# Four output tiles of the seventh image moved from the local step to other PSUM banks and an earlier place in TensorE's program

## What is computed

```python
x = x + L0(gn(x))     # 8 heads, each row of 32 tokens attends to itself
x = x + L1(gn(x))     # one head over all 1024 tokens
# L1: q = x Wq, k = x Wk (32 wide), v = x Wv (256 wide)
energy = einsum('bid,bjd->bij', k, q)
out = gamma * einsum('bij,bjc->bic', softmax(energy), v)
```

## Time and profile before

| | us |
|---|---|
| runs | 690.97, 690.84, 688.51 |
| median of the three | 690.84 |
| profiled execution, whole | 689.47 |
| its span | 687.7 |

### The profile page before, as it was taken

The page is one execution under the profiler, slowest core; times in us unless marked ns, Lnnn a source line. Parts: engine busy times, 40 slices in busy tenths (PEclk is TensorE's granted clock), DMA queues, the critical chain, the costliest instruction groups (busy, mean ns, idle before and its releaser), DMA issues.

```text
span 687.7 us, 15145 instructions
## 1 busy us (share of the span) xinstructions
PE 593.7 (86%) x5859; PEld 429.9 (63%) x5859; DVE 473.2 (69%) x765; ACT 349.5 (51%) x486; POOL 196.9 (29%) x194
## 2 busy tenths in 40 slices
PE   2475587689999999999999999999999999649987
PEld 2254265346877677757775777668776767327756
DVE  4445246868886878687868788688868794664562
ACT  2522425097518852686348652875278513651363
POOL 5602221132046023513342314420460342001203
PEclk9795798599999999999999999999999999879999
DMA  5042132212332332243042323224223132201101
GB/s 160 0 124 62 43 83 82 62 38 64 108 74 66 78 93 71 63 108 93 23 107 76 84 61 92 68 57 112 68 68 82 33 74 64 72 1 39 49 0 62
DMA packets 40308, 47.53 MB, mean 69 GB/s; under 512 B 6848, under 2 KB 32320, under 8 KB 40256
## 3 DMA queue, kind: packets, MB, share of 16 engines
q1 hardware_dynamic: 36960, 43.47, 24.0%
q10 hardware_dynamic: 3296, 3.34, 1.4%
HBM read 10.09 MB, written 8.39 MB: 27 GB/s over the span
## 4 chain that ended last, share of the span: by engine, by line
PE 64%; DVE 16%; ACT 6%; issue 5%; SPq 4%; DMA 3%; POOL 1%; ACTq 0%; DVEq 0%; POOLq 0%
PE pb L253 9%; PE pb L254 8%; PE pb L255 8%; PE pa L253 7%; PE pa L255 6%; PE pa L254 6%; PE pa L491 4%; DVE max_neg L925 4%; PE pb L557 4%; PE pa L464 3%; PE pb L539 3%; SPq L321 3%; DVE ast L827 2%; PE pa L393 2%; PE pb L393 2%
## 5 line engine op out<-in xcount | busy, mean ns | idle before, releaser
L253 PE MATMUL pb<-v_h,e_h 128*128 128x257 f16 x464 | 127.5, 275 | 0.0
L255 PE MATMUL pb<-v_h,e_l 128*128 128x257 f16 x464 | 126.5, 273 | 0.0
L254 PE MATMUL pb<-v_l,e_h 128*128 128x257 f16 x464 | 126.1, 272 | 0.0
L925 DVE TENSOR_REDUCE max_neg<-pb 128x1 f32<-128x1024 f32 x64 | 77.5, 1211 | 55.6 <-PE pb L539 55.1
L940 DVE TENSOR_TENSOR e_l<-e,e_h 128x1024 f16<-128x1024 f32 x64 | 77.8, 1223 | 17.1 <-ACT e L749 15.5
L758 ACT ACTIVATE qk_h<-pb,y_fac 128x256 f32<-128x256 f32 x58 | 27.5, 474 | 109.9 <-DVE y_fac L947 109.6
L1097 POOL TENSOR_TENSOR y<-qk_h,y 128x256 f32<-128x256 f32 x64 | 46.3, 727 | 118.1 <-ACT qk_h L758 118.0
L749 ACT ACTIVATE e<-pb,f_energy 128x1024 f32<-128x1024 f32 x64 | 71.3, 1114 | 16.1 <-PE pb L557 16.1
L1078 POOL TENSOR_TENSOR xb<-xin,bias 128x2048 f32<-128x2048 f32 x8 | 36.7, 4588 | 125.9 <-DVE x L905 125.9
L1083 POOL TENSOR_TENSOR before_turn<-before_turn,a_rinv 128x1024 f32<-128x1024 f32 x16 | 30.6, 1912 | 128.3 <-DVE a_rinv L886 128.3
L253 PE MATMUL pa<-a_nh,wqkv_h 128*128 128x512 f16 x128 | 49.9, 389 | 13.1 <-DVE before_turn L896 7.3
(11 more groups left out here) (136 smaller groups left out, 1373.4 us busy)
## 6 DMA issues: line engine op xcount, KB each, us to landing
xin<-in_x SPq DMA_DIRECT2D x16, 512.0 KB, 4.6
diag<-qkT SPq DMA_DIRECT2D x64, 128.0 KB, 2.3
diag<-turned SPq DMA_DIRECT2D x64, 128.0 KB, 2.4
turned<-before_turn SPq DMA_DIRECT2D x128, 64.0 KB, 2.0
out<-y SPq DMA_DIRECT2D x24, 256.0 KB, 2.1
out<-y ACTq DMA_DIRECT2D x8, 256.0 KB, 2.1
q_stack<-qk_hl SPq DMA_DIRECT2D x8, 128.0 KB, 2.3
k_stack<-qk_hl SPq DMA_DIRECT2D x8, 128.0 KB, 2.4
```

The source lines that it names most:

```text
L253: nc.tensor.matmul(out_ap, lh, rh, start=start, stop=False)
L254: nc.tensor.matmul(out_ap, lh, rl, start=False, stop=False)
L255: return nc.tensor.matmul(out_ap, ll, rh, start=False, stop=stop)
L925: nc.vector.tensor_reduce(max_neg[:, it:it + 1], pb[:, 0:2, :].rearrange("p a n -> p (a n)"), X, ALU.max, negate=True).then_inc(b_max, 1)
```

## The change

Output tiles 0 to 3 of image 6 are no longer made in `first` of step 7 in `pb` banks 2 and 3. They are made in `second` of step 6 in the four banks of `pa`. Tiles 0 and 1 are made key tile by key tile: key tile 0 after `b_energy_T(6, 3)`, 1 after `b_energy_T(6, 4)`, 2 after `b_energy_T(6, 5)`, 3 after `b_energy_T(6, 6)`; key tiles 4 to 6 after the last transposes of image 7 and ahead of `group_mean`; key tile 7 behind `group_mean`. Then tiles 2 and 3 follow: key tiles 0 and 1 still ahead of `group_var`, key tiles 2 to 7 behind it and ahead of `b_project_qk`. Tiles 4 to 7 of image 6 stay in `first` of step 7; tiles 4 and 5 have no wait of their own for a bank, 6 and 7 wait for the scaled results of tiles 4 and 5. `outputs_behind` also waits until image 7's local output has left `pa` (`a_ol`). For image 7, tiles 6 and 7 move from `pa` banks 0 and 1 to `pb` banks 0 and 1, and wait for its last exponential instead of for its scaled tiles 0 and 1.

```diff
@@ result_bank
+        def next_to_last(b):
+            return isinstance(b, int) and b == IMAGES - 2
+
         def result_bank(b, it):
 
             if last_image(b):
-                it = it % 6
-                return pa[:, it, :] if it < 4 else pb[:, it - 2, :]
+                return pa[:, it, :] if it < 4 else pb[:, (it - 2) % 4, :]
+            if next_to_last(b) and it < 4:
+                return pa[:, it, :]
             return pb[:, 2 + it % 2, :]
@@ b_output
                     pe.wait_ge(b_el, nth(b, 8, jts[-1] + 1))
 
                     if it >= 6:
-                        pe.wait_ge(b_part, nth(b, 8, it - 5))
+                        pe.wait_ge(b_exp, nth(b, 8, 8))
+                elif next_to_last(b) and it < 4:
+                    pe.wait_ge(b_el, nth(b, 8, jts[-1] + 1))
+                elif next_to_last(b):
+                    if it >= 6:
+                        pe.wait_ge(b_part, nth(b, 8, it - 1))
                 elif jts[0] == 0:
@@ first, TensorE
-                    if o and not last_image(i - 1): b_output(i - 1, it, b, range(0, 4))
+                    if o and b and not next_to_last(i - 1): b_output(i - 1, it, b, range(0, 4))
                     if b and it == 2: b_energy(i, 1, m)
-                    if o and not last_image(i - 1): b_output(i - 1, it, b, range(4, 8))
+                    if o and b and not next_to_last(i - 1): b_output(i - 1, it, b, range(4, 8))
@@ outputs_behind
-            def outputs_behind(b, jts):
+            def outputs_behind(b, jts, its=range(6)):
 
                 for jt in jts:
                     if jt == 0:
 
                         pe.wait_ge(b_vl, nth(b, 4, 4))
-                    for it in range(6):
+                        pe.wait_ge(a_ol, nth(IMAGES, 2, 0))
+                    for it in its:
                         b_output(b, it, False, (jt,))
@@ second, TensorE
                 if last_image(i): outputs_behind(i, (0,))
+                if next_to_last(i): outputs_behind(i, (0,), (0, 1))
                 if b: b_energy_T(i, 4)
                 if b and f: b_project_v(i, (3,))
                 if last_image(i): outputs_behind(i, (1,))
+                if next_to_last(i): outputs_behind(i, (1,), (0, 1))
                 if f: a_project_qk(i + 2, 1, (1,))
                 if b: b_energy_T(i, 5)
                 if last_image(i): outputs_behind(i, (2,))
+                if next_to_last(i): outputs_behind(i, (2,), (0, 1))
                 if m: a_projection(i + 1, f, (0, 1))
                 if b: b_energy_T(i, 6)
                 if last_image(i): outputs_behind(i, (3,))
+                if next_to_last(i): outputs_behind(i, (3,), (0, 1))
                 if m: a_projection(i + 1, f, (2,))
@@
                 if m: transposes("b", i + 1, (2, 3))
                 for j in range(4):
+                    if next_to_last(i) and j == 0: outputs_behind(i, (4, 5, 6), (0, 1))
                     if m and j == 2: group_var("b", i + 1)
                     if f: a_project_v(i + 2, (j,))
                     if m and j == 0: group_mean("b", i + 1)
+                    if next_to_last(i) and j == 0:
+                        outputs_behind(i, (7,), (0, 1))
+                        outputs_behind(i, (0, 1), (2, 3))
+                    if next_to_last(i) and j == 2: outputs_behind(i, range(2, 8), (2, 3))
```

## The result

| | before | changed |
|---|---|---|
| median of 11 runs each | 688.3 us | 692.79 us |
| lowest, highest | 687.47, 690.97 | 691.28, 696.6 |
| span of the profiled execution | 687.7 | 692.3 |

The ratio is 1.006, with a 95% interval from 1.0043 to 1.0078: the change costs some 4.1 us. The two spans differ by 4.6 us; the working's sum on the span was +3.9.

The account below looks back on a forecast made before the run. TensorE was busy 86%, but step 7's start hung on a DMA chain and the maxima. Terms -1.5 + 4.5 - 1.5 + 2.4 = +3.9 us, on the runs' middle of 690.2: 694.1 us, range 691.0 to 696.5.

Parts of the forecast that it names:

- (a, b): Step 6's first hole: key tiles 0 to 3 of tiles 0 and 1 let the mean come 1.5 us earlier.
- the likeliest case: Step 6's first hole: added key tiles keep the clock full, so the projection's 24 matmuls gain 2.16 us.
- The other bound, 0.5: Step 6's first hole: the clock falls all the same but returns sooner; the mean comes only 0.5 us earlier.
- (c): Image 7's norm: variance matmul queued behind the last split and 18 matmuls at half clock, +4.5 us.
- (d): Behind the variance: 36 matmuls under cover cost nothing, and the query/key projection at full clock gains 1.5 us.
- (e): First half of step 7: without cover TensorE idles 5.4 us, then energies and tile 4 meet half clock; +2.4 us.
- the bound I gave: Step 7, tile 4 all at half clock: 5.1 us, making that stretch's sum +3.2 us.
- (f): From energy 4 on: order unchanged, image 7's tiles 6 and 7 in other banks cost nothing; 0.
- the kept clock in the norm: Rival: filled holes keep the clock full through image 7's norm, 2.6 instead of 4.5 us; sum +2.0, 692.2 us; chance 0.22.
- Full clock everywhere: Rival: norm and step 7's energies 0 to 3 also at full clock; sum -1.5, 688.7 us; chance 0.08.
- the clock falling at both holes: Rival: clock falls in both step 6 holes, part of the 36 matmuls delays the projection; about +6, 696.2 us; chance 0.15.
- no moved tile waited before the projection: Against the rival that a moved tile's late wait leaves step 6's holes unfilled and lengthens them; little chance.

Follow-up runs that it names:

- early variance: Changed kernel with image 7's variance matmul put ahead of key tile 7 and all of tiles 2 and 3; ratio 1.0018 to the kernel before, +1.2 us.
- three tiles: Against the kernel before: tiles 0 to 2 in step 6, variance matmul ahead of key tile 7, step 7 laid out anew; ratio 0.9916, 5.8 us under.
- The experiment on the kernel before: Kernel before, no tile moved, with a wait for the last split and 18 thrown-away matmuls ahead of the variance matmul; ratio 1.0064, +4.4 us.
- the kernel with fillers between the energies: Changed kernel plus 48 thrown-away matmuls ahead of energy 0 and 12 behind each of energies 0, 1, 2; ratio 1.0012 to the kernel before.
- the two faster kernels: Two or three tiles moved to step 6, variance matmul ahead of key tile 7, step 7 laid out anew; ratios 0.9927 and 0.9916 to the kernel before.
- the kernel with 48 fillers: Changed kernel plus 48 thrown-away matmuls between the query/key projection and step 7's first energy; ratio 1.0052 to the kernel before.

## Why the prediction was right, step by step

The forecast was slower, 694.1 us in 691.0 to 696.5, and 692.79 was measured. The sum of +3.9 stands against 4.1 by the ratio and 4.6 by the spans. The absolute number lies 1.3 us high because I started from 690.2, and the kernel before measured 688.3 over more runs. That the sum came so near is in part luck: its terms missed by +0.7, -0.4, +0.1, +0.7 and -0.4 us, and two of them hang on when the clock came back in this one execution.

(a, b) The key tiles filled the hole without a wait of their own, and the projection ran at full clock, as said. But the likeliest case, that the clock doesn't fall in this hole, did not come, and the size was half: -0.77 instead of -1.5. The clock fell earlier than before, near 590, ahead of the first added matmul (591.20), and came back near 593.5. So transposed energies 3 and 4 ran at half clock; the next one, at full clock again, is the third row:

```profile
590.38 1.03 PE L561 MATMUL pb<-k_stack,q_stack 98*128 98x512 f16 x2 [2.38 <-ACT e L768]
...
592.62 1.03 PE L561 MATMUL pb<-k_stack,q_stack 98*128 98x512 f16 x2
...
594.86 0.60 PE L561 MATMUL pb<-k_stack,q_stack 98*128 98x512 f16 x2 [0.54 <-ACT e L768]
```

They start 2.24 us apart instead of 1.81, key tile 2 ends late, and the projection starts at 595.96 instead of 595.21. Its 24 matmuls then gain the 2.16 us. In the traces of the first and the last but one experiment above (early variance, and three tiles) the clock didn't fall there at all; the distance from the third transposed energy to the mean is 20.1 us in both, against 21.6 before: the full 1.5 us. In the changed kernel it is 20.8. Seven traces here have the added key tiles in this hole. In five of them the clock fell before the first added matmul had begun, 2.7 to 3.4 us after the third transposed energy, and the distance is 20.5 to 20.8 us; in the two in which it was still full then, it stayed so. In the three traces without the key tiles it fell later, 4.0 to 5.5 us after that energy. So the added matmuls may keep the clock, but in five of these seven executions they came too late for it, and 1.0 us is nearer to the usual gain than 1.5. The other bound, 0.5, covered it.

(c) Right: +4.12 instead of +4.5, since the clock returned within the 18 matmuls (3.65 us from the first of them to the variance, not 3.83) and the variance itself was then 0.28 us long. The experiment on the kernel before gives +4.5 for this distance alone.

(d) Right in size: -1.43 instead of -1.5, of which the 36 matmuls earned some 0.9 by the experiment with (c) alone. The 36 matmuls took 3.9 us of the cover, and the second half of the projection waited for its split, as said (0.66 us idle before 621.02).

(e) The mechanism held, the size was 0.7 us short. Steps of 2.43 us between energies 0 and 3 stand against 2.45. The step that was mis-sized is tile 4: I let the clock return 4.5 us after energy 3's start, and it returned 6.1 us after it, near 641.3. The tile ran at half clock throughout, 5.2 us, which was the bound I gave. From energy 3 to 4 it is 5.96 us instead of 5.3. This miss belongs to the one execution: in the trace of the early variance, with the same program in step 7, the clock was back 4.4 us after energy 3, energy 3 to 4 took 5.20 us, and (e) was +2.3.

The Trainium skill's rule on bursts separated by waits (TensorE: Matmul & The Clock Gate, "HAM oscillation — how this bites in real kernels") names the cost that decides (e). The trace agrees with it: after the 5.4 us of waiting the energies ran at 0.50. By a steady clock (e) would have been -1.1, and the kernel with fillers between the energies shows just that.

(f) -0.4 instead of 0. I put it down to the low clock in the second half of step 7, which met other matmuls; that is not shown by itself. With both sets of banks the distance from energy 7 to the end is 42.9 to 43.3 us in the traces in which the clock falls there (the changed kernel's 42.9 among them, 43.3 before) and 41.6 to 41.7 in the three in which it doesn't, so a single execution's time hangs by some 1.5 us on that.

Of the rivals, the kept clock in the norm would have shown 1.00 in the window of the 18 matmuls; it shows 0.54. Full clock everywhere needed it in the energies; they show 0.50. Of the clock falling at both holes the first half came true in part, as told under (a, b); the second did not, since the 36 matmuls ran at 1.00. And no moved tile waited before the projection: the only wait of one in the changed kernel is key tile 7's for the last split, 2.0 us, which is part of (c).

## What to carry to other kernels

Before moving work off a busy engine, ask what that work was covering: here 10.6 us of matmuls lay, all but 1.1 us, in the shade of a DMA chain and of a chain of row maxima. Moving work out paid where a piece was longer than its shade, which is where the two faster kernels take most of their gain from. When independent work is put into a hole of an in-order engine, put it behind the small instructions that a serial chain on other engines waits for, not ahead of them. And idle time of TensorE can cost twice: here the work that followed it ran at half clock. Matmuls that compute nothing won 3.3 us back in a thin stretch, though only what the change had lost there; 18 of them ahead of the variance cost 4.4 us. So such a filler must lie in the shade of a wait, and ahead of nothing that a chain needs.

## What the runs showed of the hardware

With one pair of 512-column matmuls every 2.0 us and no idle time over 1.41 us between them, the granted clock fell near 632.2, in the third pair, after two pairs at 1.00 (the kernel with 48 fillers). With 12 matmuls of 257 columns in each of the three gaps it stayed at 1.00. When the clock returned under dense matmuls differed: 3.5 us after the first of the 18 matmuls in the norm of the changed kernel, 5.3 us after the first of tile 4 in its step 7, 3.6 us after the first of the same tile 4 in the trace of the early variance; and the 18 fillers of the kernel with (c) alone went by in 3.84 us without its return. The same program finds the clock back sooner or later from execution to execution.
